# Six layers of windowed attention and gated FFN: the layer loop written out, a new order of work in each slot, and cross-attention logits in pairs

## The reference, cut to what matters

```python
x = x + tanh(g_xattn) * xattn(layernorm(x), ctx)      # 16 heads of 8; logits + per-head bias of clip(frac_k - frac_q)
z = layernorm(x)
for i in range(6):
    q, k, v = split(shift_tokens(z) @ Wqkv[i])        # 16 heads of 64
    q, k = rotary(l2norm(q) * qs), rotary(l2norm(k) * ks)
    # windows of 32 queries see 64 keys: their own window and the one before, banded
    z = z + local_softmax_attention(q, k, v) @ Wo[i]
    z = z + (a * gelu(gate)) @ W2[i] + b2[i]          # a, gate = layernorm(shift_tokens(z)) @ W1[i] + b1[i]
x = x + tanh(g_ffn) * z
```

## Time and profile before

| | us |
|---|---|
| median of 3 runs | 2065.31 (2059.34 to 2075.24) |
| the profiled execution, its time | 2061.48 |
| its span, first to last instruction | 2059.7 |
| PE busy | 1797.2 |
| DVE busy | 1600.0 |
| ACT busy | 1384.6 |
| POOL busy | 1332.1 |
| mean granted TensorE clock | 0.972 of 2.4 GHz |

### The profile page before, as it was taken

One profiled execution on the slowest core, in us unless ns is written; L12 is line 12 of the kernel. 1 busy time (PEld: TensorE's weight loads), 2 busy tenths in 40 slices (PEclk: granted clock), 3 DMA queues, 4 the chain that ended last, 5 costly groups with the idle time before them and its releaser, 6 DMA issues.

```text
span 2059.7 us, 86637 instructions
## 1 busy us (share of the span) xinstructions
PE 1797.2 (87%) x33584; PEld 1401.8 (68%) x33584; DVE 1600.0 (78%) x3772; ACT 1384.6 (67%) x3701; POOL 1332.1 (65%) x1226
## 2 busy tenths in 40 slices
PE   6999878998879898789988899988898988899887
PEld 3445457777667776677776677776677776677766
DVE  5766679898468987488896589885689885689984
ACT  3677657777557776567775577775577775577765
POOL 3444467777467777377775477774677773677773
PEclk9999979999989999999999999999899999899999
DMA  5000021111021111111110211110211110211111
GB/s 121 4 5 5 1 70 33 35 37 32 25 64 41 31 36 28 63 34 33 40 31 23 68 40 31 41 31 23 64 44 31 31 42 22 65 37 37 31 33 46
DMA packets 59120, 77.81 MB, mean 38 GB/s; under 512 B 16608, under 2 KB 31674, under 8 KB 57914
## 3 DMA queue, kind: packets, MB, share of 16 engines
q1 hardware_dynamic: 58938, 75.36, 13.9%
HBM read 22.63 MB, written 1.05 MB: 11 GB/s over the span
## 4 chain that ended last, share of the span: by engine, by line
PE 60%; DVE 15%; issue 12%; ACT 6%; POOL 5%; SPq 0%; DMA 0%; DVEq 0%; ACTq 0%; POOLq 0%
PE proj_ps L455 7%; PE s_ps L476 7%; PE tr_ps L465 7%; PE y_ps L524 7%; PE proj_ps L457 5%; PE proj_ps L456 5%; PE y_ps L516 4%; DVE by_cos L1091 3%; PE pv_ps L506 3%; ACT square L816 3%; DVE by_sin L1091 3%; DVE xs L1352 3%; PE s_ps L571 3%; DVE sumsq L1103 2%; PE s_ps L691 2%
## 5 line engine op out<-in xcount | busy, mean ns | idle before, releaser
L1502 POOL TENSOR_TENSOR qk<-by_cos,by_sin 128x512 f32<-128x512 f32 x388 | 495.3, 1276 | 208.3 <-DVE by_sin L1091 201.9
L1509 POOL TENSOR_TENSOR qk<-qk,inv_norm 128x512 f32<-128x512 f32 x388 | 404.8, 1045 | 68.7 <-ACT inv_norm L822 41.6
L1091 DVE TENSOR_TENSOR by_cos<-proj_ps,tab 128x512 f32<-128x512 f32 x364 | 249.4, 685 | 159.6 <-ACT square L816 158.6
L816 ACT ACTIVATE square<-proj_ps 128x512 f32<-128x512 f32 x364 | 217.4, 597 | 195.1 <-PE proj_ps L457 194.8
L1515 POOL TENSOR_TENSOR s_sb<-s_sb,row_max 128x512 f32<-128x512 f32 x192 | 202.7, 1056 | 136.1 <-DVE row_max L1122 136.1
L455 PE MATMUL proj_ps<-w_hi,x_hi 128*128 128x512 f32 x546 | 273.8, 502 | 4.8 <-DVE by_sin L1091 2.6
L465 PE MATMUL tr_ps<-ident,qk 128*128 128x128 f32 x1544 | 247.2, 284 | 24.2 <-ACT x_hi L810 11.8
L1103 DVE TENSOR_REDUCE sumsq<-square 128x8 f32<-128x512 f32 x388 | 262.2, 676 | 0.0
L1091 DVE TENSOR_TENSOR by_sin<-proj_ps,tab 128x512 f32<-128x512 f32 x364 | 247.8, 681 | 0.0
L465 PEld LDWEIGHTS tr_ps<-ident,qk 128*128 128x128 f32 x1544 | 184.0, 146 | 72.5 <-POOL qk L1509 28.5
L457 PE MATMUL proj_ps<-w_hi,x_lo 128*128 128x512 f32 x546 | 222.1, 407 | 0.0
(11 more groups left out here) (172 smaller groups left out, 4167.1 us busy)
## 6 DMA issues: line engine op xcount, KB each, us to landing
arena<-v SPq DMA_DIRECT2D x388, 130.0 KB, 2.4
w_raw<-in_L_ffn_Wqkv SPq DMA_DIRECT2D x7, 1536.0 KB, 7.3
wo<-in_L_ffn_Wo SPq DMA_DIRECT2D x7, 512.0 KB, 3.8
w_raw<-in_L_ffn_W SPq DMA_DIRECT2D x7, 341.0 KB, 5.5
c_in<-in_ctx SPq DMA_DIRECT2D x16, 64.0 KB, 1.8
xn<-in_fside_BxS SPq DMA_DIRECT2D x1, 1024.0 KB, 6.0
out<-z SPq DMA_DIRECT2D x4, 256.0 KB, 3.0
w<-in_L_ffn_W SPq DMA_DIRECT2D x12, 64.0 KB
```

The lines of the kernel that those rows point to most:

```text
L1091: return dve.tensor_tensor(dst[:, c % 2, :].rearrange("p (h d) -> p h d", d=DH), ps, tb, ALU.mult)
L1502: pool.tensor_tensor(heads(qk[:, c, :]), heads(by_cos[:, c % 2, :]), heads(by_sin[:, c % 2, :])[:, :, ::-1, :], ALU.add).then_inc(qk_added, 1)
L1509: pool.tensor_tensor(ap, ap, inv_norm[:, c, :].unsqueeze(2).to_broadcast([128, 8, DH]), ALU.mult).then_inc(qk_ready, 1)
```

## The change

The layer loop becomes a Python loop on all five engines: the six layers are written out, so that their semaphore counts are constants outside the loop over pairs of slots, which stays a hardware loop of six iterations in each layer. In `scores` and `values`, windows 0 and 1, which see the same 64 keys, become one matmul with 64 queries: three matmuls for each head and pair instead of four. `xs` holds only the shifted half; `ln_stats` takes statistics of the two halves in two instructions, the first straight from z, and `ln_apply` writes two halves. The order of work in a slot is another on PE, ACT, DVE and POOL. In the x stage `x_scores` is called twice a slot and makes two groups: bias and logits of g, then logits and bias of g + 1. The diff leaves out further lines with the same edit of the layer loop and of the `xs_ready` counts.

```diff
+QUERIES = [(slice(0, 2 * WINDOW), 1), (slice(2 * WINDOW, 3 * WINDOW), 2), (slice(3 * WINDOW, 4 * WINDOW), 3)]
...
-xs = sb("xs", [128, 2, D])
+xs = sb("xs", [128, 2, D // 2])
...
-stats = sb("stats", [128, 2, 6])
+stats = sb("stats", [128, 2, 2, 6])
...
-    with sp.Fori(1, LAYERS + 1) as L:
+    for L in range(1, LAYERS + 1):
...
             for r in range(2):
-                for w in range(NT // WINDOW):
-                    feat, toks = slice(64 * r, 64 * r + 64), slice(WINDOW * w, WINDOW * w + WINDOW)
+                for toks, w in QUERIES:
+                    feat = slice(64 * r, 64 * r + 64)
                     mm = pe.matmul(s_ps[toks, slot_of(r, w), 64 * a:64 * a + 64], q_T[par][feat, PAIRS * h + a, toks],
                                    k_T[par][feat, PAIRS * h + a, keys_of(w)], start=True, stop=True)
...
-                for w in range(NT // WINDOW):
-                    i, toks = slot_of(r, w), slice(WINDOW * w, WINDOW * w + WINDOW)
+                for toks, w in QUERIES:
+                    i = slot_of(r, w)
                     keys = slice(64 * i, 64 * i + 64)
                     src = v_mid[:, par] if w == 2 else v_swap[:, par] if r else v[par][:, 0]
                     mm = pe.matmul(pv2_ps[toks, r, (DH + 1) * a:(DH + 1) * (a + 1)], p_T[keys, h, a, toks],
...
         if i == 0:
-            pe.wait_ge(xs_ready, T * 2)
+            pe.wait_ge(xs_ready, T)
...
@@ -553,22 +556,32 @@
...
+    def x_bias(T, par, g, first):
+        hi, lo = flat(pos_hi[:, GH * g:GH * g + GH]), pos_lo[g]
+        pe.matmul(s_ps[:, g % 2, :], d_hi[:, par], hi, start=first, stop=False)
+        pe.matmul(s_ps[:, g % 2, :], d_hi[:, par], lo, start=False, stop=False)
+        return pe.matmul(s_ps[:, g % 2, :], d_lo[:, par], hi, start=False, stop=not first)
+    def x_logits(T, par, g, first):
+        rows = slice(32 * g, 32 * g + 32)
+        return pe.matmul(s_ps[:, g % 2, :], xq[rows, par, :], flat(xk_bd[rows, par]), start=first, stop=not first)
     def x_scores(T, par, g):
         if g == 0:
             pe.wait_ge(d_split, T + 1)
         if not after(T, 1):
-            pe.wait_ge(diag_ready, g + 1)
+            pe.wait_ge(diag_ready, g + 2)
         if after(T, 1) or g >= 2:
             pe.wait_ge(masked, T * 4 + (g - 1))
-        hi, lo = flat(pos_hi[:, GH * g:GH * g + GH]), pos_lo[g]
-        pe.matmul(s_ps[:, g % 2, :], d_hi[:, par], hi, start=True, stop=False)
-        pe.matmul(s_ps[:, g % 2, :], d_hi[:, par], lo, start=False, stop=False)
-        pe.matmul(s_ps[:, g % 2, :], d_lo[:, par], hi, start=False, stop=False)
+        x_bias(T, par, g, True)
         if g == 0:
             pe.wait_ge(xk_ready, T + 1)
-        rows = slice(32 * g, 32 * g + 32)
-        pe.matmul(s_ps[:, g % 2, :], xq[rows, par, :], flat(xk_bd[rows, par]), start=False, stop=True).then_inc(s_full, 1)
+        if after(T, 1) or g >= 2:
+            pe.wait_ge(masked, T * 4 + g)
+        x_logits(T, par, g, False).then_inc(s_full, 1)
+        x_logits(T, par, g + 1, True)
+        x_bias(T, par, g + 1, False).then_inc(s_full, 1)
...
@@ -597,8 +610,6 @@
...
-        if not first:
             x_p_transpose(T - 1, 3)
         if front_on:
             x_project(T + 1)
...
-        x_scores(T, par, 3)
         x_p_transpose(T, 1)
         x_values(T, par, 0)
...
-    with pe.Fori(1, LAYERS + 1) as L:
+    for L in range(1, LAYERS + 1):
...
         def slot(T, n, par, first=False, behind=2, front_on=True, last_front=False):
             if first:
                 pe.wait_ge(z_ready, L * NF + (NB - NF))
             scores(T, par, 0)
             if front_on:
                 project(T + 1, 0)
             if behind >= 1:
                 p_transpose(T - 1, 1)
-            if behind >= 2:
-                shift_state(T - 2, tile_of(z, n - 2, D // 2))
+            if front_on:
+                project(T + 1, 1)
             if first:
                 qk_transpose(T, 2)
             qk_transpose(T, 3)
-            if front_on:
-                project(T + 1, 1)
+            if behind >= 2:
+                shift_state(T - 2, tile_of(z, n - 2, D // 2))
             if behind >= 1:
                 values(T - 1, 1 - par, 1)
+            if front_on:
+                project(T + 1, 2)
+            if behind >= 1:
                 att_transpose(T - 1, 0)
-            if front_on:
-                project(T + 1, 2)
+            scores(T, par, 1)
+            if not front_on:
+                f_transpose(0, tr_ps)
+            if front_on:
+                project(T + 1, 3)
                 qk_transpose(T + 1, 0)
-            scores(T, par, 1)
-            if front_on:
-                project(T + 1, 3)
-            else:
-                f_transpose(0, tr_ps)
-            p_transpose(T, 0)
             if behind >= 1:
                 att_transpose(T - 1, 1)
+            p_transpose(T, 0)
             if front_on:
                 project(T + 1, 4)
                 qk_transpose(T + 1, 1)
+                project(T + 1, 5)
             values(T, par, 0)
-            if front_on:
-                project(T + 1, 5)
-                if not last_front:
-                    x_transpose(T + 2)
+            if front_on and not last_front:
+                x_transpose(T + 2)
             if behind >= 1:
                 out_project(T - 1, L)
...
             if not first:
                 norms(T, 3)
             if front_on:
                 square_chunk(T + 1, 0)
             if behind >= 1:
                 p_out(T - 1, 1)
+            if front_on:
+                square_chunk(T + 1, 1)
             if first:
                 qk_out(T, par, 2)
             qk_out(T, par, 3)
-            exps(T, 0)
             if front_on:
                 norms(T + 1, 0)
-                square_chunk(T + 1, 1)
             if behind >= 1:
                 att_out(T - 1, 0)
             if front_on:
                 v_out(T + 1, 1 - par, 0)
+            exps(T, 0)
+            if not front_on:
+                f_out(0, tr_ps)
+            if front_on:
+                square_chunk(T + 1, 2)
+                norms(T + 1, 1)
                 qk_out(T + 1, 1 - par, 0)
-            if front_on:
-                norms(T + 1, 1)
-                square_chunk(T + 1, 2)
-            else:
-                f_out(0, tr_ps)
-            p_out(T, 0)
+            if behind >= 1:
+                att_out(T - 1, 1)
             if behind >= 2:
                 ln_std(T - 2, par)
-            if behind >= 1:
-                att_out(T - 1, 1)
+            p_out(T, 0)
+            if front_on:
+                qk_out(T + 1, 1 - par, 1)
+                square_chunk(T + 1, 3)
+                norms(T + 1, 2)
+            if front_on and not last_front:
+                x_out(T + 2)
             if front_on:
                 v_out(T + 1, 1 - par, 1)
-                qk_out(T + 1, 1 - par, 1)
             exps(T, 1)
-            if front_on:
-                norms(T + 1, 2)
-                square_chunk(T + 1, 3)
-                if not last_front:
-                    x_out(T + 2)
+            if front_on:
                 qk_out(T + 1, 1 - par, 2)
...
-    with dve.Fori(1, LAYERS + 1) as L:
+    for L in range(1, LAYERS + 1):
         def add_out(T, n):
             dve.wait_ge(y_full, T + 1)
             zt = tile_of(z, n)
             dve.tensor_tensor(zt, zt, y_ps[:, 0:D], ALU.add).then_inc(z_attn, 1)
         def ln_stats(T, n, par):
-            zt = tile_of(z, n, 0, D // 2)
             dve.wait_ge(sh_full, T + 1)
-            dve.tensor_scalar(xs[:, par, 0:D // 2], zt, 1.0, None, ALU.mult).then_inc(xs_ready, 1)
-            dve.tensor_copy(xs[:, par, D // 2:D], y_ps[:, 0:D // 2]).then_inc(xs_ready, 1)
-            dve.wait_ge(xs_ready, T * 2 + 2)
-            dve.bn_stats(stats[:, par], xs[:, par]).then_inc(stat_done, 1)
+            dve.tensor_copy(xs[:, par], y_ps[:, 0:D // 2]).then_inc(xs_ready, 1)
+            dve.bn_stats(stats[:, par, 0], tile_of(z, n, 0, D // 2))
+            dve.wait_ge(xs_ready, T + 1)
+            dve.bn_stats(stats[:, par, 1], xs[:, par]).then_inc(stat_done, 1)
         def ln_variance(T, par):
-            dve.bn_aggr(mean_var[:, par], stats[:, par]).then_inc(var_ready, 1)
+            dve.bn_aggr(mean_var[:, par], flat(stats[:, par])).then_inc(var_ready, 1)
         def ln_apply(T, n, par):
             dve.wait_ge(rstd_ready, T + 1)
-            dve.tensor_scalar(tile_of(xn, n), xs[:, par],
-                              mean_var[:, par, 0:1], rstd[:, par:par + 1], ALU.subtract, ALU.mult).then_inc(xn_ready, 1)
-        def step(T, g, behind=2, front_on=True, stats_ready=None):
-            Tn, hn = (T, 0) if g == 3 else (T - 1, 1)
-            norm_on = g == 3 or g == 1 and behind >= 1
-            if g % 2 == 0:
-                mask(T, g // 2)
-                row_maxima(T, g // 2)
-            if front_on:
-                times_cos(T + 1, g, L - 1)
-                times_sin(T + 1, g, L - 1)
-                sum_squares(T + 1, g)
```

(104 more changed lines are left out.)

5 lines of the change are left out of this document (3 added, 2 removed).

## The result

The changed kernel takes 3475.06 us (median of 4 runs, 3458.55 to 3491.96), the kernel before 2064.48 beside it: a ratio of 1.68, 95% interval 1.672 to 1.693. The prediction was 1915, range 1860 to 1990. The measured time lies outside on the slow side, beyond even the 2420 to 3030 of the third rival, whose mechanism it is.

What follows compares the result with a forecast made beforehand. Steady slots were taken as bound by a 15.38 us loop in which PE and DVE wait for each other. 2061.5 - 97 - 32 - 19 = 1913.5, with half the distance to the median 1915 us; range 1860 to 1990.

Steps and rivals of the forecast that it cites:

- third rival: In scores and values: 16 changes of tile shape a call slow the kernel to 2420 to 3030 us; chance 0.13.
- Three matmuls instead of four: In scores and values: 48 records take three quarters of the time, 0.59 us a call, 0.20 less.
- The order: Steady slots: PE's 1.33 us wait goes; with smaller calls and LayerNorm, slot 14.2 us, -97 us over 84 slots.
- The LayerNorm: DVE in a slot: copy -0.77, second statistics +0.25, second ln_apply half +0.3; work falls from 13.9 to 13.7 us.
- The change of layer: Between layers, five times: first mask 5.0 us earlier, 1.5 from the clock; -6.5 us each, -32 in all.
- second rival: Layer changes and pair loops: the code fetch stays or grows, kernel 1930 to 2013 us; chance 0.07.
- The x stage: Paired logits overlap and save 1.4 us a slot over 15 slots; -19 us, between -4 and -30.
- first rival: Steady slots: the new order finds a new wait, slot near 15.0 us, kernel 1980 us; chance 0.14.

Runs made afterwards that it cites:

- uniform kernel: Changed kernel with two matmuls of 64 queries per head and pair, all one tile shape (attention not the reference's): 1875.51 us, ratio 0.909.
- four-window kernel: Changed kernel with the four windows of 32 queries back in scores and values, everything else of the change kept: 1918.4 us, ratio 0.929.
- unrolled kernel: Kernel before with only the layer loop written out in Python on all engines: 2023.55 us, ratio 0.979.
- by-pair kernel: Changed kernel with each call's 24 matmuls reordered: per head pair both 64-query ones, then four of 32: 2384.22 us, ratio 1.155.
- by-size kernel: Changed kernel with each call's 24 matmuls reordered: all eight of 64 queries first, then sixteen of 32: 2039.2 us, ratio 0.988.

## Why the prediction was wrong, step by step

**Three matmuls instead of four: the step that failed.** I put -0.20 us on a call; it is +3.1 to +3.3. From "62 loads take 0.89 us at the lower clock and 64 take 0.70 at full" I concluded that handing out instructions sets the time, and scaled by the count of records. Even as a price of records this was too much: the uniform kernel shows 0.16 for half of them. But above all the count isn't what the edit changed. It brought a second tile shape into a loop of one, and the trace had rows with a price for that, 0.1 to 0.2 us. I set them aside because in those rows the new tile lies over the old one, and here beside it. No row supported that reservation. It was an excuse that decided the sign, held at 0.87 against 0.13. The break-even was 0.03 us a change; the price is 0.14 to 0.19, some five times that.

**The third rival held**, just above its price: net of the 0.2 saved it gave 1.4 to 3.0 more for a call, measured 3.1 to 3.3. It still fell 445 us short of the result, since it priced a slot at full clock. By its own sum a slot has 14 + 4 x 3.1 = 26.4 us of PE work; measured are 29.9. The rest is the lower clock, for a third of the span where before it was 6%: of the 15.55 us that a slot is longer than in the four-window kernel, 4 x 3.23 = 12.9 are calls by their medians, 2.6 is everything else on PE. Both stretch with the clock: the 226 calls that run wholly at a granted 1.00 take 3.90 (`scores`) and 3.92 us (`values`), the 42 at the lower level 6.0 to 6.1. The Trainium skill's sentence ("TensorEngine Tiling (Array Packing)", Key Properties) that changing the tiling mode and not just the tile drains the engine fits what the runs show, 0.145 to 0.149 us from the last start of one shape to the first of the other, with no reservation for tiles that don't overlap.

**The order: right in its mechanism, and closer in its number than it deserves.** Predicted slot 14.2, measured 14.39 with calls of 0.79. The 14.2 holds 0.4 from smaller calls, which didn't come; without them its sum is 14.6. The loop is the one drawn from the earlier trace rows. The chain of waits through a steady slot of the four-window kernel (start, us, what):

```profile
1180.06 0.69 DVE by_cos L1094
...
1185.60 0.21 ACT log_sq L825
...
1185.83 0.22 ACT inv_norm L827
...
1186.19 1.05 POOL qk L1522
...
1187.29 0.65 PE tr_ps L468 x4
...
1191.47 0.44 PE tr_ps L468 x4
...
1194.42 0.69 DVE by_cos L1094
```

From the cosine product to the end of the scale 7.18 us (predicted 7.2), on to the last transpose 4.2 (predicted 3.8 with a smaller call, 4.0 without), to the next cosine product 2.95 (predicted 3.1 with a smaller call, 3.3 without, and a hand-over of 0.1). Only the way to the norm differs: it goes over PE's projection and one small call, not over DVE alone. PE's wait of 1.33 us behind `xs` is gone, as said. With the old layer loop and x stage this is 2065 to 1966: -99 us, predicted -97. That agreement is luck: 84 slots of 0.96 less are 81 us, and the other 18 fall in the remaining parts, mainly slot 0 (16.6 to 15.1) and the change of layer (64.8 to 63.4), which I left as they are.

**The LayerNorm: a wrong reason that cost nothing.** I let DVE's work fall from 13.9 to 13.7 us. DVE's busy time over the span rose, 1600.0 to 1615.0, because the wait for POOL moved to `ln_apply`, where I had put 0.3 and a second half. I had read the 762 against the minimum of 143 correctly as waiting, and then didn't ask, in my own terms, what that wait would meet next. In the old order it costs 47 us, in the new one nothing.

**The change of layer: right.** -6.5 each predicted; -7.7 each by the unrolled kernel, and -41 us in all against -32. The first mask comes 2.2 us after the start of PE's last transposes (1149.28 to 1151.50); before it was 7.1 (from 1163.03, a row not shown, to the earlier trace rows): 4.9 less, predicted 5.0. The clock of the 10.4 us behind it stays at 1.00. The second rival (the stop belongs to new code, or the pair loops pay for it) is refuted by the same run.

**The x stage: the sign right, the term wrong, the rest luck.** 10 to 12 us, not 19. The overlap came in full, but the step from it to 1.4 us in each of 15 slots failed: behind it PE waits for POOL and ACT, and the lower clock in some slots takes back the 0.5 us that is left. The twelve steady slots measure 0.0 less (13.45 to 13.43). The gain goes with the upper clock level, which PE reaches at 30.9 us instead of 50.8, and which I hadn't thought of.

**The first rival** (a new wait, 1980 us) didn't come: -99 us for the order leaves no room for it.

Without the merge the sum -97 - 32 - 19 = -148 stands against a measured -146. That these meet is partly luck too, since -97 counts the smaller calls and leaves out slot 0, -32 measured -41, and -19 measured -10 to -12. The miss of the whole is the one term that was put at 0.2 us a call.

## What to carry to other kernels

Fewer matmuls isn't less time: before merging small matmuls, ask whether the merged ones keep the tile shape of their neighbours, and if they can't, sort a batch by shape (2039 us against 3475 for the same work) or leave it (1918 us). A row that carries a price for the very thing an edit introduces may be set aside only on the strength of another row. And an instruction that is long because it waits for another engine can't be won by deleting it: look for the next instruction of its kind that will meet that engine. The version to keep is the changed kernel with four windows, 1918 us, 7.1% faster than before.

## What the runs showed that I had not expected

- A change between 64 by 64 and 64 by 32 tiles costs 0.14 to 0.19 us of a call, on disjoint parts of the array. Start to start over the change it is 0.145 to 0.149 us in every order, 0.24 at the lower clock.
- The granted clock falls on a PE that the trace shows as 100% busy: from 1.00 to 0.94 and 0.79 in the windows above, behind calls of 48 small matmuls that take 4 us. In the by-pair kernel, with half the changes, its mean is 0.972, as before, and in the by-size kernel 0.984; so the clock went with how often the shape changes, though the busy share by the records is 97, 94 and 93% in the changed, the by-pair and the by-size kernel. What the chip takes for activity the runs don't show.
- Leaving out a DVE instruction of 762 ns lengthened a slot from 15.36 to 16.04 us, since what it waited for was met elsewhere.
- A loop over layers cost 7.7 us at each jump back: some 3.3 and 1.6 us of idle PE, and the half clock behind them.
- With the logits in pairs PE reached the upper clock level 20 us earlier at the start of the kernel. The gain of the pairs lies there; the steady x slots are as long as before.
